# Score maxima from the high fp16 halves alone, in two row groups at once, in a two-layer cross-attention and expert kernel

## The reference

```python
q = (query @ Wq + bq).reshape(B, Nq, H, D).transpose(0, 2, 1, 3)
k = (key_value @ Wk + bk).reshape(B, Nkv, H, D).transpose(0, 2, 1, 3)
v = (key_value @ Wv + bv).reshape(B, Nkv, H, D).transpose(0, 2, 1, 3)
attn = jnp.einsum('bhqd,bhkd->bhqk', q, k) * scale
attn = jnp.clip(attn, -CLAMP, CLAMP)
attn = jax.nn.softmax(attn, axis=-1)
x = jnp.einsum('bhqk,bhkd->bqhd', attn, v).reshape(B, Nq, Cq)
```

## Time and profile before

| | us |
|---|---|
| median of 3 runs | 242.64 |
| lowest, highest | 242.48, 245.16 |
| profiled execution: time | 242.7 |
| profiled execution: span | 240.8 |
| busy in the span: PE, DVE, ACT, POOL | 199.2, 142.6, 93.7, 97.3 |

### The profile page before, as it was taken

The page is one execution under the profiler, slowest core; times in us unless marked ns, Lnnn a source line. Parts: engine busy times, 40 slices in busy tenths (PEclk is TensorE's granted clock), DMA queues, the critical chain, the costliest instruction groups (busy, mean ns, idle before and its releaser), DMA issues.

```text
span 240.8 us, 3547 instructions
## 1 busy us (share of the span) xinstructions
PE 199.2 (83%) x1189; PEld 117.8 (49%) x1197; DVE 142.6 (59%) x530; ACT 93.7 (39%) x222; POOL 97.3 (40%) x107
## 2 busy tenths in 40 slices
PE   1697589998899969999899899988787987777760
PEld 0443235444454446726564367643235866666650
DVE  5899836832877297957655698788884621111110
ACT  2251135615262266315652433246763433322320
POOL 0428805200022502171209137650017768878743
PEclk9999999999999999999999999999999999999995
DMA  6510111100110000129920001210002322323222
GB/s 198 160 65 25 32 48 49 49 0 10 53 28 0 3 1 0 46 79 297 336 80 15 34 3 44 88 48 4 0 1 56 37 27 42 45 34 48 33 26 29
DMA packets 15193, 13.07 MB, mean 54 GB/s; under 512 B 3520, under 2 KB 12161, under 8 KB 15169
## 3 DMA queue, kind: packets, MB, share of 16 engines
q1 hardware_dynamic: 11440, 10.17, 13.5%
q0 software_dynamic: 3008, 2.31, 6.8%
q10 hardware_dynamic: 721, 0.30, 0.5%
HBM read 7.99 MB, written 3.21 MB: 47 GB/s over the span
## 4 chain that ended last, share of the span: by engine, by line
PE 36%; DVE 29%; POOL 10%; DMA 9%; issue 9%; ACT 5%; POOLq 1%; DVEq 0%; ACTq 0%
DMA out<-pT,idx 7%; PE psum L949 7%; POOL out L1848 5%; DVE rden L1456 4%; DVE mrow L1436 4%; PE psum L862 3%; PE psum L905 3%; DVE pT L1593 3%; PE psum L931 2%; DVE stats L1314 2%; PE psum L933 2%; PE psum L872 2%; PE psum L982 2%; DVE xn L1421 2%; PE psum L986 2%
## 5 line engine op out<-in xcount | busy, mean ns | idle before, releaser
L734 ACT ACTIVATE pT<-psum 103x512 f32<-103x512 f32 (+1 forms) x48 | 28.3, 598 | 39.1 <-PE psum L933 38.9
L1757 POOL TENSOR_SCALAR ve<-mv 128x4 f32<-128x4 f32 (+1 forms) x19 | 4.4, 229 | 95.5 <-DVE mv L1317 95.4
L862 PE MATMUL psum<-c 128*128 128x512 bf16 x115 | 29.4, 379 | 1.6 <-ACT key_map L758 1.0
L1436 DVE TENSOR_REDUCE mrow<-psum 128x4 bf16<-128x308 f32 x64 | 27.3, 468 | 5.4 <-PE psum L905 5.2
L1848 POOL DMA_INDIRECT out<-pT,idx x16 | 25.5, 1594 | 10.2 <-DVE pT L1660 6.8
L1840 POOL DMA_INDIRECT pT<-gather_rows,idx x16 | 17.7, 1106 | 23.7 <-DVE idx L1647 19.5
L1658 DVE TENSOR_TENSOR pT<-psum,b_rows 128x256 f32<-128x256 f32 (+1 forms) x9 | 3.5, 394 | 35.8 <-PE psum L1270 35.8
L905 PE MATMUL psum<-k_stack,q_stack 128*128 128x308 f16 x64 | 16.4, 298 | 6.3 <-DVE mrow L1436 5.8
L1258 PE MATMUL psum<-xinT,w 128*128 128x256 f32 (+1 forms) x72 | 16.2, 368 | 4.3 <-ACT xinT L818 3.6
L931 PE MATMUL psum<-q_stack,k_stack 128*103 128x512 f16 (+1 forms) x48 | 18.8, 393 | 0.5 <-DVE mT L1441 0.5
L1456 DVE RECIPROCAL rden<-psum 128x512 f32<-128x512 f32 (+1 forms) x5 | 13.6, 2713 | 9.6 <-PE psum L949 9.6
(11 more groups left out here) (197 smaller groups left out, 378.2 us busy)
## 6 DMA issues: line engine op xcount, KB each, us to landing
w<-in_L_ffn_W SPq DMA_DIRECT2D x16, 256.0 KB, 5.8
gather_rows<-xrow SPq DMA_DIRECT2D x4, 272.0 KB, 2.1
x<-in_x SPq DMA_DIRECT2D x4, 256.0 KB, 4.2
out<-res SPq DMA_DIRECT2D x4, 256.0 KB, 2.0
q_stack<-q_hi SPq DMA_DIRECT2D x24, 32.0 KB, 1.8
q_stack<-q_lo SPq DMA_DIRECT2D x24, 32.0 KB, 1.8
b_rows<-in_L_ffn_b SPq DMA_DIRECT2D x1, 512.0 KB, 3.6
pT<-gather_rows,idx POOLq DMA_INDIRECT x16, 2.6
```

Source lines behind the costliest of these rows:

```text
L734: nc.scalar.activation(pT[0:n, b % 2, s, :], ST_ps[s % 2][0:n, :], ACT.Exp).then_inc(exp_done, 1)
L862: pe.matmul(bank[b][:, :], ident16, c16[:, 0:4 * P], start=True, stop=True)
L1436: dve.tensor_reduce(mrow[:, b % 2, j, g * GH:(g + 1) * GH], S_ps[u % 2][:, 0:GK].rearrange("p (h k) -> p h k", h=GH), X, ALU.max).then_inc ...
```

## The change

1. **Maxima from the high parts.** `scores` no longer reads `q_stack` and `k_stack`. It takes the 32 rows of a head group from `q_hi` and from a new tile `k_max` (the scaled float32 keys `kT`, rounded to fp16 and masked), and does two head groups one behind the other in different row groups of TensorE, into two banks. One reduction on VectorE then takes 8 heads' maxima from both banks. 8 pairs for a batch replace 16 units. In the opening pairs alternate between banks 0, 1 and 2, 3; afterwards all use banks 0 and 1, so a pair waits until the one before is read. The maximum is only a shift of the exponent.
2. **Batch 0's query stack by transfers.** `w_q4`, `b_q4` and the four-fold query product go. Batch 0 gets `q_hi` and `q_lo` like the others and its stack by 16 transfers: eight issued by SyncE, four by ScalarE, four by GpSimd.
3. **Keys in two parts.** The four-fold keys of batch 0 are made first (77 columns a group), those of batches 1 to 3 later; VectorE's low parts for these move to slot 3 of phase 0. `kT` is made in the opening.
4. **Order.** GpSimd normalises batch 1; its six loads go to SyncE; statistics and norm of batch 2 and `q_low(1)` move from the opening to the start of phase 0; in phase 0 `prep_T` and `prep_q` of batch 2 move from slots 1, 2 to 4, 5 and `values` from slot 3 to 2. Warming matmuls are put at TensorE's start and behind the context transposes, and are changed elsewhere.
5. The check on the numbers' reach, among the experts, has other limits and one more small VectorE operation.

```diff
-        w_q4 = sb("w_q4", [P, G, 4, GD])
-        b_q4 = sb("b_q4", [P, G])
+        k_max = sb("k_max", [P, B, GH, NK], F16)
...
+        kT_ps = bank[0][:, 0:B * NK]
+        k4_first = tail2_ps[:, 0:G * NK].rearrange("p (g k) -> p g k", g=G)
+        LATER = (B - 1) * NK
+        k4_later = psum[:, 5:7, 0:2 * LATER].rearrange("p u (g n) -> p u g n", g=2)
...
+        def stacked(eng, b):
+            eng.wait_ge(q_stack_done[b], 192 if b == 0 else 256)
+            if b == 0:
+                eng.wait_ge(q_stack_low, 64)
+        def prep_slot(b):
+            return 4 if b == 0 else 1
+        def values_slot(b):
+            return 2 if b == 0 else 3
+        def score_bank(b, u):
+            return 2 * (u % 2) if b == 0 else 0
...
 SyncE, behind the small loads
+            for n, (w, bias) in enumerate((("L0_xattn_Wv", "L0_xattn_bv"), ("L1_xattn_Wk", "L1_xattn_bk"), ("L1_xattn_Wv", "L1_xattn_bv"))):
+                sp.dma_start(w_kv[0:DC, n + 1, :], a[w]).then_inc(ld_kv, 16)
+                sp.dma_start(w_kv[DC:DC + 1, n + 1, :], a[bias].rearrange("(o d) -> o d", o=1)).then_inc(ld_kv, 16)
+            stack_queries(0)
...
 ScalarE, opening
+            act.wait_ge(kT_ps_done, 1)
+            nc.scalar.activation(kT[:].rearrange("p b k -> p (b k)"), kT_ps, ACT.Copy, scale=float(HD) ** -0.5).then_inc(kT_done, 1)
+            act.wait_ge(k4_ps_done, 1)
+            nc.scalar.activation(k_parts[:, :, 0, :], k4_first, ACT.Copy, scale=float(HD) ** -0.5).then_inc(k_hi_done, 1)
             copy_T(0, 0, prep_ps)
...
+            q_high(0)
+            act.wait_ge(q_lo_done, 1)
+            for g in range(G):
+                act.dma_start(q_stack[2 * GD:3 * GD, 0, g, :], q_lo[g * GD:(g + 1) * GD, 0, :]).then_inc(q_stack_done[0], 16)
             copy_T(0, 1, prep_ps)
+            act.wait_ge(k4_ps_done, 2)
+            nc.scalar.activation(k_parts[:, :, 1:, :].rearrange("p (u g) b k -> p u g (b k)", g=2), k4_later, ACT.Copy,
+                                 scale=float(HD) ** -0.5).then_inc(k_hi_done, 1)
             q_high(1)
...
 TensorE
+            def scores(b, u):
+                if u == 0:
+                    pe.wait_ge(q_hi_done, b + 1)
+                    pe.wait_ge(k_max_done, 1 if b == 0 else 2)
+                if b >= 1:
+                    pe.wait_ge(max_done, b * PAIRS + u)
+                elif u >= 2:
+                    warm_head(3)
+                    pe.wait_ge(max_done, u - 1)
+                j, g0, to = u // 2, u % 2 * 2, score_bank(b, u)
+                for k in range(2):
+                    rows = slice((g0 + k) * GD, (g0 + k + 1) * GD)
+                    pe.matmul(bank[to + k][:, 0:GK], q_hi[rows, b % 2, j * P:(j + 1) * P], k_max[rows, b].rearrange("p h k -> p (h k)"),
+                              start=True, stop=True, tile_position=((g0 + k) * GD, 0)).then_inc(s_ps_done, 1)
...
+            warm_early(7, 2)
             pe.wait_ge(ld_ctx, 16)
...
+            warm_early(4, 2)
...
+            pe.matmul(kT_ps, w_kv[:, 0, :], ctxT[:, :, 0:NK], start=True, stop=True).then_inc(kT_ps_done, 1)
             pe.wait_ge(w_4_done, 1)
             for g in range(G):
+                ins = pe.matmul(k4_first[:, g, :], w_k4[:, g].rearrange("p r d -> p (r d)"), ctxT[:, 0, 0:NK], start=True, stop=True)
+            ins.then_inc(k4_ps_done, 1)
+            prep_T(0)
+            keys_later(0)
+            prep_q(0)
+            keys_later(1).then_inc(k4_ps_done, 1)
+            pe.wait_ge(k_lo_done, 1)
+            for u in range(PAIRS):
+                scores(0, u)
+                if u == 3:
                     prep_T(1)
+                if u == 5:
                     prep_q(1)
+                if u % 2 == 1 and u >= 5:
+                    maxima_T(0, (u - 5) // 2)
...
 VectorE
+            def maxima(b, u):
+                dve.wait_ge(s_ps_done, 2 * (b * PAIRS + u + 1))
+                to, h0 = score_bank(b, u), u % 2 * 2 * GH
+                dve.tensor_reduce(mrow[:, b % 2, u // 2, h0:h0 + 2 * GH].rearrange("p (c h) -> p c h", c=2),
+                                  psum[:, to:to + 2, 0:GK].rearrange("p c (h k) -> p c h k", h=GH), X, ALU.max).then_inc(max_done, 1)
...
+                q_low(0)
+                for u in range(PAIRS):
+                    maxima(0, u)
...
                         if s == 0:
                             maxima_out(b)
+                            if b == 0:
+                                q_low(1)
+                                ln0_stats(2)
...
+                        if b == 0 and s == 2:
+                            ln0_apply(2)
+                        if b == 0 and s == 3:
+                            keys_low(1, B, k4_later)
...
 GpSimd
+            ln_rstd(0, 0, 0)
+            pool.wait_ge(kT_done, 1)
+            mask_keys(0, 1)
+            ln_rstd(0, 1, 1)
+            for j in range(J):
+                ins = nc.gpsimd.tensor_scalar(xn[:, j, :], x[:, J + j, :], mv[:, 0, j, 0:1], rstd[:, 0, j:j + 1], ALU.subtract, ALU.mult)
+            ins.then_inc(xn_done, 1)
+            pool.wait_ge(q_lo_done, 1)
+            for g in range(G):
+                pool.dma_start(q_stack[3 * GD:, 0, g, :], q_lo[g * GD:(g + 1) * GD, 0, :]).then_inc(q_stack_low, 16)
+            pool.wait_ge(k_lo_done, 1)
+            stack_keys(0)
+            mask_keys(1, B)
```

More of the change, by code:

```diff
@@ L39 @@
 CLAMP = 1e4
-PART_MAX = 256.0
+QUERY_MAX, KEY_MAX = 128.0, 16.0
 ROW = D + E
@@ L613, in _, with stack_queries @@
             sp.dma_start(bs_rows[:], a["L1_ffn_bs"].rearrange("(o d) -> o d", o=1).broadcast_to([P, E])).then_inc(ld_rt, 16)
+            for n, (w, bias) in enumerate((("L0_xattn_Wv", "L0_xattn_bv"), ("L1_xattn_Wk", "L1_xattn_bk"), ("L1_xattn_Wv", "L1_xattn_bv"))):
+                sp.dma_start(w_kv[0:DC, n + 1, :], a[w]).then_inc(ld_kv, 16)
+                sp.dma_start(w_kv[DC:DC + 1, n + 1, :], a[bias].rearrange("(o d) -> o d", o=1)).then_inc(ld_kv, 16)
+            def stack_queries(b):
+                for r, (part, split) in enumerate(((q_hi, q_hi_done), (q_hi, q_hi_done), (q_lo, q_lo_done), (q_lo, q_lo_done))):
+                    if b == 0 and r >= 2:
+                        continue
+                    if r % 2 == 0:
+                        sp.wait_ge(split, b + 1)
+                    for g in range(G):
+                        sp.dma_start(q_stack[r * GD:(r + 1) * GD, b, g, :],
+                                     part[g * GD:(g + 1) * GD, b % 2, :]).then_inc(q_stack_done[b], 16)
+            stack_queries(0)
             sp.dma_start(tile_rows[:], a["c_rows"]).then_inc(ld_rc, 16)
@@ L617, in _ @@
             sp.dma_start(b2_rows[:], a["L1_ffn_b2"].rearrange("(o e) d -> o e d", o=1).broadcast_to([P, E, D])).then_inc(ld_b2, 16)
-            def stack_queries(b):
-                for r, (part, split) in enumerate(((q_hi, q_hi_done), (q_hi, q_hi_done), (q_lo, q_lo_done), (q_lo, q_lo_done))):
-                    if r % 2 == 0:
-                        sp.wait_ge(split, b)
-                    for g in range(G):
-                        sp.dma_start(q_stack[r * GD:(r + 1) * GD, b, g, :],
-                                     part[g * GD:(g + 1) * GD, b % 2, :]).then_inc(q_stack_done[b], 16)
             stack_queries(1)
@@ L848, in warm_head, with warm_early @@
             def warm_head(n):
-                src = k_parts[:].rearrange("p g b k -> p (g b k)")
                 for _ in range(n):
-                    pe.matmul(bank[2][:, :], src[:, 0:P], src[:, 0:4 * P], start=True, stop=True)
+                    pe.matmul(tail2_ps[:, 2 * P:4 * P], ident16, c16[:, 0:2 * P], start=True, stop=True)
+            def warm_early(n, b):
+                for _ in range(n):
+                    pe.matmul(bank[b][:, :], mT[:, 0, 0:P], mT[:, 0, :], start=True, stop=True)
             def warm_prep(n):
@@ L887, in prep_q @@
                 pe.matmul(prep_ps[:, :], w_q[:, 0, :], xnT[:, 0, :], start=True, stop=True).then_inc(q_ps_done, 1)
-            def scores(b, j, groups=range(G)):
-                if j == 0 and groups[0] == 0:
-                    if b >= 1:
-                        pe.wait_ge(q_stack_done[b], 256)
-                    if b == 0:
-                        pe.wait_ge(k_lo_done, 2)
-                        warm_head(10)
-                    pe.wait_ge(k_stack_done, b + 1)
-                for g in groups:
-                    u = (b * J + j) * G + g
-                    if b == 0 and j == 0 and g % 2 == 0:
-                        pe.wait_ge(q4_lo_done, g // 2 + 1)
-                    if u >= 2:
-                        if b == 0:
-                            warm_head(1)
-                        pe.wait_ge(max_done, u - 1)
-                    pe.matmul(S_ps[u % 2][:, 0:GK], q_stack[:, b, g, j * P:(j + 1) * P],
-                              k_stack[:, b, g].rearrange("p h k -> p (h k)"), start=True, stop=True).then_inc(s_ps_done, 1)
+            def scores(b, u):
[12 more added lines that the diff above has]
```

(10 more changed lines are left out.)

214 lines of the change are left out of this document (89 added, 125 removed).

## The result

The changed kernel takes 236.5 us, the median of six executions; the kernel before took 242.45 in six beside them. The ratio is 0.974, with a 95% interval of 0.971 to 0.977: a gain of 6 us. Forecast were 233.7 us in a range of 229.5 to 238.5.

The account below looks back on a forecast made before the run. VectorE was taken to bound the opening and TensorE the phases. From 242.7 us, 12.5 came off in the opening, 2.4 went back in phase 0 and 1.1 in phases 1 and 2: 233.7 us, range 229.5 to 238.5.

Parts of the forecast that it names:

- Opening: Stage ahead of phase 0: relieving VectorE brings the first score product to 20.1 from 32.56, a gain of 12.5 us.
- eight maxima back to back on VectorE: Sign in the opening: batch 0's eight reductions run without gaps ahead of the first score product at 20.1 (18.5 to 23).
- rival a: Opening: GpSimd's work or descriptors, or SyncE's queue, replace the maxima as limit, 1 to 3 us late; 235.5 us, chance 0.15.
- The lock: Opening: GpSimd's `k_max` beside VectorE's norm of batch 0 excludes it for whole instructions; 0.4 us added, between 0 and 0.6.
- The early matmuls: Opening: warming matmuls, seven and four, put TensorE at its upper clock from 7 us; otherwise steps are 2 us longer.
- Phase 0: First phase: batch 1's maxima on one bank pair, 1.2 us a turn, make it 21.4 us, giving back 2.4.
- rival (e): TensorE's clock falls after idling in phase 0 and stays low in phases 1 and 2; slower than before, chance 0.03.
- the likeliest case: The whole kernel: the forecast itself, 233.7 us, with 232 to 236 counted as its span; chance 0.50.
- The pairs: Phases 1 and 2: row-group switching makes each pair 0.38 us on TensorE, 0.12 more, 1.9 us for sixteen.
- (c): All 24 row-group pairs cost much more, drained in and out, weight loads unhidden: 0.63 us each; 239.7 us, chance 0.08.
- (d): The two halves of a row-group pair run one after the other, 0.13 us more, 16 times; 235.8 us, chance 0.08.
- (b): Pairs in row groups cost nothing to enter: 229.7 us, or 229 if phase 0 is tight too; chance 0.14.

Follow-up runs that it names:

- e_warm02: Changed kernel with warming matmuls in phase 0's idle stretches and eight more in slot 5 of phase 2; 233.49 us, ratio 0.956.
- e_full: Changed kernel with the maxima of batches 1 to 3 from two full 128-row products, no row groups (other scores); 234.46 us, ratio 0.965.
- e_pad: Changed kernel with one extra full 308-column matmul, result overwritten, ahead of each pair of batches 1 to 3; 239.14 us, ratio 0.977.
- e_best: Changed kernel with pairs 1, 3, 5 of batch 1 in banks 5 and 6, and warming matmuls in phases 0 and 2; 233.13 us, ratio 0.955.
- e_bestfull: e_best with the maxima of batches 1 to 3 from two full 128-row products instead of row groups (other scores); 233.46 us, ratio 0.963.
- e_warm0: Changed kernel with warming matmuls filling TensorE's idle stretches in phase 0 only; 235.05 us, ratio 0.968.
- r_after: The changed kernel as it is, run and profiled once more beside the variants; 236.53 us, ratio 0.974.
- b_early: Kernel before the change with only the eleven early warming matmuls added at TensorE's start; 244.13 us, ratio 1.001.

## Why the prediction was near, and where its terms were off

**Opening: right within 0.7 us.** Forecast: first score product at 20.1. Measured: 20.78, 11.8 us before. The steps, in the changed kernel: product for `kT` done at 7.1 (forecast 7.2), transposes of `xn` to 9.3 (9.1), query product to 11.1 (10.9), `q_hi` to 11.9 (11.6), `q_lo` to 12.8 (12.4). VectorE's timeline for the rest:
```profile
7.05 1.50 DVE L1461 TENSOR_SCALAR xn<-x,mv,rstd 128x128 f32<-128x128 f32 x4 [0.60 <-POOL rstd L1790]
...
12.70 2.91 DVE L1475 TENSOR_REDUCE mrow<-psum 128x8 bf16<-128x616 f32 x4
15.85 1.50 DVE L1475 TENSOR_REDUCE mrow<-psum 128x8 bf16<-128x616 f32 x2 [0.25 <-PE psum L933]
18.40 1.50 DVE L1475 TENSOR_REDUCE mrow<-psum 128x8 bf16<-128x616 f32 x2 [1.04 <-PE psum L933]
```
A reduction over both banks takes 0.79 us and 0.70 back to back, as worked out. It is not VectorE alone that paces them: ahead of the fifth and the seventh it waits for TensorE, 0.25 and 1.04 us, where batch 1's transposes, query product and warming matmuls lie between the pairs. I had put 0.8 there. From 13.5 to 20.2 us the chain of waits lies on TensorE alone, and 2.8 us of it are warming matmuls (L878), among them:
```profile
13.85 0.43 PE psum L878 x3
...
19.21 0.76 PE psum L878 x6
```
So eight maxima back to back on VectorE, the sign I had named, came only for the first four; whether fewer warming matmuls would shorten the opening or lose the clock wasn't tried. The queues weren't late (rival a): the chain of waits has neither a DMA nor GpSimd in it from 12.8 to 20.8. The last transfer into batch 0's `q_stack` landed at 18.3, and GpSimd's `k_stack`, the later of the two, ended at 19.06:
```profile
16.79 2.27 POOL L1803 TENSOR_TENSOR k_stack<-k_parts,c 128x1232 f16<-128x1232 f16 x1
```
That is 1.7 us ahead of the first score product, where I had put a cover of 0.8 to 1.1.

**The lock: right.** The norm takes 1.50 us, not 1.11, and this row of GpSimd's timeline lies in its midst:
```profile
7.69 0.78 POOL L1822 TENSOR_TENSOR k_max<-kT,c 128x308 f16<-128x308 f32 x1 [0.68 <-ACT kT L703]
```
In e_warm02, e_full and e_pad, where `k_max` comes only at 7.98 to 8.49, behind most or all of the norm, the norm takes 1.10 to 1.12; in e_best `k_max` comes at 7.48, in its midst, and it takes 1.60. 0.4 to 0.5 us were 0.4 in the sum. The rule of the Trainium skill (SBUF — State Buffer, section "Who interferes with whom") agrees with these rows.

**The early matmuls: right.** Put at 2 us; 2.6 in the start of phase 0 and 2.5 in the time (239.08, one execution, against 236.53).

**Phase 0: the right pace, a wrong clock.** Forecast 21.4 us, paced by the maxima of a single pair of banks, 1.2 us a turn. In e_warm02, at the upper level, it has 21.8 and 1.23 a turn, and e_best, which doubles the banks, 20.6. In the kernel as changed it has 23.4. The step that failed is the assumption that the upper level stays through the thin stretch: I named the falling clock as rival (e), took it for a matter of whole phases with a chance of 0.03, and rested on the 1.00 of the earlier trace rows, one execution with an idle stretch of 1.66 us and not four stretches in ten us. It came in small: phase 0 is 1.6 us longer than e_warm02's and phase 2 is 1.3, 2.9 in all. Without them the changed kernel stands at 236.5 - 2.9 = 233.6. That e_warm02's median is 233.5 is no proof of it, as the kernel before took 244.6 on that chip and 242.5 here: by the ratios, 0.974 and 0.956, the fill is worth 1.8%, some 4.4 us. The 236.5 us lie in the stated range, but above the 232 to 236 of the likeliest case, and what put them there is (e), which the range was to leave out: that the range held is owed to the fall being short.

**The pairs: a term that was mis-sized.** I took 0.38 us for a pair, 0.12 more than two full products in series, from the way in and out of the column groups: 1.9 us. Way in and pair were about right (0.10 and 0.23), but behind full products the next matmul comes 0.36 later, and not 0.26, where it isn't a score product. By the rows of e_best and e_bestfull a pair costs TensorE between 0.07 more and 0.02 less than two full products: nothing. So (c) and (d) fall, and of (b) only that the pair costs no more than before, not that it saves. The saving of 0.8 on VectorE didn't come either; in its place the turn of 1.23 us showed in phase 1 too (second pair 1.23 us behind the first, 0.87 before; sixth behind fifth 1.23 and 0.98). Forecast for both phases +1.1, measured at the upper level +0.4: two terms that were both wrong made up for each other in part, which is luck. With phase 0's +2.8 in place of +2.4 and the opening's 11.8 in place of 12.5 that makes 242.7 - 11.8 + 2.8 + 0.4 = 234.1, 0.6 from e_warm02's median.

**What stays open.** Why the clock falls in phase 2 of some kernels and not of others: e_warm0 and r_after have the same work and the same idle 2 us there, and the one keeps 2.4 GHz, the other loses it at 83.5 for 3.4 us. The stretch of 24 us in the executions named at the start lies in the same place and is as little explained (the one of the changed kernel has 6.8 us at 1.2 GHz in phase 1 as well); and b_early shows low stretches in a kernel whose neighbour, the kernel before, has none in its profile. The kernel before isn't free of them either, it seems: on r_after's chip its longest execution, 244.57 us, was granted 0.973 in the mean, the others 0.987 to 0.990. Which executions have them is partly chance. The stretch in phase 2 stands in r_after's timeline behind this wait:
```profile
82.10 0.30 PE L933 MATMUL psum<-k_max,q_hi 32*128 32x308 f16 x2 [2.07 <-DVE mrow L1475]
...
84.14 0.44 PE L933 MATMUL psum<-k_max,q_hi 32*128 32x308 f16 x2
```
The kernel before had a wait of 1.86 us at this place and no fall. Nor is it settled how much of the gain of e_best over e_warm02 outlives the spread of their executions.

## What to carry to other kernels

When a change takes work from the engine that bounds a stage, ask what it does to the idle time of TensorE: fill what is left with matmuls that nobody waits for, but not so many that they hold up the next product, and look at the durations of one known instruction through the whole stage, not at the mean clock. Row groups with a short contraction aren't a gain by themselves when the neighbours use the full array: measure from the matmul ahead to the matmul behind. And two banks that are read and written in turn cost a full round trip each time, wherever VectorE is the pace.
